# Weighing of the normed rows for the second half of the heads as three fp32r products, with the softmax sums of that slot behind its scores

## The reference

```
h1 = adaln(x, t, norm1_w, norm1_b)
x = mha(h1, h1, attn1_wq, attn1_wk, attn1_wv, attn1_wo, attn1_bo) + x
h2 = adaln(x, t, norm2_w, norm2_b)
x = mha(h2, context, attn2_wq, ...) + x
h3 = adaln(x, t, norm3_w, norm3_b)
x = glu_ff(h3, ff_w1, ff_b1, ff_w2, ff_b2) + x
...
def mha(xq, ctx, wq, wk, wv, wo, bo):
    scores = einsum('bhqd,bhkd->bhqk', q, k) / sqrt(DH)
    attn = softmax(scores, axis=-1)
    out = einsum('bhqk,bhkd->bhqd', attn, v)
    return out.transpose(0, 2, 1, 3).reshape(b, sq, INNER) @ wo + bo
...
attn = softmax(q[..., :, None] * k[..., None, :], axis=-1)   # router of the expert layer
logits = einsum('bsej,bsj->bse', attn, v)
```

## Time and profile before

| | us |
|---|---|
| median of 3 runs | 2139.29 |
| lowest and highest | 2135.04, 2143.15 |
| the profiled execution, its own time | 2140.15 |
| its span in the trace | 2138.4 |
| PE busy | 2045.5 (96%) |
| DVE, ACT, POOL busy | 1321.4, 1394.0, 1071.4 |
| one round of the loop (chunk to chunk in the trace, the PE of 1016.64 to 1121.52) | 104.88 |
| mean granted clock of TensorE, share of full | 0.989 |

### The profile page before, as it was taken

How to read it: one execution, slowest core, us unless ns; L and a number is a source line. 1 busy time by engine, 2 the same in 40 slices (tenths; PEclk the granted TensorE clock), 3 DMA queues, 4 the chain that set the end, 5 groups by cost and what they waited for, 6 DMA issues and landing times. The chain is left out here.

```text
span 2138.4 us, 38742 instructions
## 1 busy us (share of the span) xinstructions
PE 2045.5 (96%) x11068; PEld 1339.2 (63%) x11068; DVE 1321.4 (62%) x3389; ACT 1394.0 (65%) x2665; POOL 1071.4 (50%) x1198
## 2 busy tenths in 40 slices
PE   7899999999999999999999999999999888799996
PEld 5455555555555556555555555555565557699996
DVE  5554657676767666666666666666666555455565
ACT  4566666676767676767676767676766656666663
POOL 2434443636373737373737373737364355456654
PEclk9999999999999999999999999999999999999998
DMA  5110111111111111111212121111112212122266
GB/s 152 45 25 25 50 35 50 46 50 47 52 44 49 44 49 44 50 48 48 53 42 59 34 59 40 53 48 46 50 50 74 73 54 59 48 55 71 62 186 211
DMA packets 136322, 127.36 MB, mean 60 GB/s; under 512 B 14665, under 2 KB 110569, under 8 KB 136234
## 3 DMA queue, kind: packets, MB, share of 16 engines
q1 hardware_dynamic: 127466, 109.11, 18.5%
q0 software_dynamic: 8768, 17.20, 2.5%
HBM read 86.63 MB, written 40.67 MB: 60 GB/s over the span
## 5 line engine op out<-in xcount | busy, mean ns | idle before, releaser
L1882 POOL TENSOR_TENSOR pr<-pr,sm 128x512 f32<-128x512 f32 x256 | 277.6, 1097 | 484.9 <-DVE sm L1428 484.9
L1105 ACT ACTIVATE kp<-ps 128x512 f32<-128x512 f32 x512 | 298.9, 601 | 179.5 <-PE ps L283 175.0
L823 PE MATMUL ps<-tt,V 128*128 128x512 f32 x768 | 382.0, 595 | 3.5 <-ACT tt L1105 3.5
L1418 DVE TENSOR_REDUCE mx<-ps 128x8 f32<-128x512 f32 x256 | 176.8, 691 | 308.1 <-PE ps L772 308.1
L1105 ACT ACTIVATE tt<-ps 128x512 f32<-128x512 f32 x512 | 275.2, 591 | 40.2 <-PE ps L802 40.1
L772 PE MATMUL ps<-kp,hf 128*64 128x256 f32 x2048 | 279.3, 394 | 5.3 <-DVE pr L1421 2.4
L283 PE MATMUL ps<-cT,M 128*128 128x512 f32 x768 | 262.1, 464 | 0.0
L772 PEld LDWEIGHTS ps<-kp,hf 128*64 128x64 f32 x2048 | 125.4, 137 | 196.7 <-DVE pr L1421 140.2
L1105 ACT ACTIVATE pt<-ps 128x512 f32<-128x512 f32 x256 | 153.6, 600 | 143.0 <-PE ps L784 140.7
L283 PE MATMUL ps<-hk,M 128*128 128x512 f32 x768 | 242.2, 438 | 0.0
L929 PE MATMUL ps<-xT,wt 128*128 128x128 f32 (+1 forms) x1728 | 221.4, 278 | 9.5 <-DVE wt L1709 5.0
(11 more groups left out here) (229 smaller groups left out, 3477.2 us busy)
## 6 DMA issues: line engine op xcount, KB each, us to landing
mod<-emb_s SPq DMA_DIRECT2D x96, 256.0 KB, 4.2
xr<-rows_s SPq DMA_DIRECT2D x144, 66.0 KB
cb<-y_s SPq DMA_DIRECT2D x32, 256.0 KB
x_in<-in_x_dram SPq DMA_DIRECT2D x16, 256.0 KB, 4.3
xn_s<-x_in SPq DMA_DIRECT2D x16, 256.0 KB, 2.1
res<-xn_s SPq DMA_DIRECT2D x16, 256.0 KB, 2.8
c_in<-in_ctx_dram SPq DMA_DIRECT2D x16, 256.0 KB, 4.8
y_s<-res SPq DMA_DIRECT2D x16, 256.0 KB, 2.0
```

The lines of the kernel that those rows point to most:

```text
L823: mm = nc.tensor.matmul(psO[:], Vw[a][:, g * HG + head_at(h), :], tt[:, h, :], start=(g == 0 and h == 0), stop=ends)
L1105: return nc.scalar.activation(o, i, ACT.Copy)
L1418: nc.vector.tensor_reduce(mx[:, p % 2, :], heads(psS[p % 2][:]), AX_X, ALU.max).then_inc(max_done, 1)
L1882: tensor(v, v, sm[:, p, :].unsqueeze(2).broadcast_to([P, HG, 64]), ALU.mult).then_inc(prob_done, 1)
```

## The change

The weighing of unit 1 (in slot 2, for all chunks but the last) is done as three fp32r products instead of one fp32 product. For this, pt and h_tm are needed as an upper and a lower part each:

- ACT copies psT to pt_hi (fp32r) where it copied to pt. DVE makes the lower part, pt_lo = psT - pt_hi (`turn_rest`), once for each of the four steps, ahead of `peak` of the same step. psT is free only after that, so `turn` of steps 1 to 3 waits for pt_rest instead of pt_done.
- In slot 0, ACT makes a second copy of h1 (h_hl, upper part) and DVE the lower part (`tm_lower`, at h = 3).
- PE: lower h x pt_hi, upper h x pt_hi, upper h x pt_lo, each for both halves of the rows.
- In slot 2, none of the four `total` stands in the first part any more; they stand at h = 0, 1, 2 and 3.
- In the table of slot 2, `ln_lo(c, 2)` goes from h = 3 to h = 2 and `router_sum` from h = 2 to h = 3. At one h the jobs of the table stand ahead of `total`.

```diff
+            h_hl = sb("h_hl", [P, 2, NT, D], F32R, halves)
+            pt_hi, pt_lo = (sb(f"pt_{k}", [P, 2, CT], F32R, halves) for k in ("hi", "lo"))
...
+        def in_halves(i, u):
+
+            return u == 1 and not c_last(i)
+
+        def turned(i, u, p):
+
+            return (pt_rest, 4 * i + p + 1) if in_halves(i, u) else (pt_done, 4 * seq(i, u) + p + 1)
...
             def turn(i, u, p):
 
                 n = 4 * seq(i, u) + p
-                if not (isinstance(n, int) and n < 1):
+                if p:
+                    wait(turned(i, u, p - 1))
+                elif not (isinstance(n, int) and n < 1):
                     pe.wait_ge(pt_done, n)
...
                 pst = pstw[p % 2]
+                if in_halves(i, u):
+                    if p == 0:
+                        pe.wait_ge(tm_rest, i + 1)
+                    for k, of in enumerate((1, 0)):
+                        for s in range(2):
+                            rows = slice(64 * s, 64 * s + 64)
+                            nc.tensor.matmul(pst[s][:], h_hl[rows, of, p, :], pt_hi[rows, p % 2, :], start=k == 0, stop=False)
+                    pe.wait_ge(pt_rest, 4 * i + p + 1)
+                    for s in range(2):
+                        rows = slice(64 * s, 64 * s + 64)
+                        nc.tensor.matmul(pst[s][:], h_hl[rows, 0, p, :], pt_lo[rows, p % 2, :], start=False, stop=True).then_inc(t_done, 1)
+                    return
...
-                copy(pt[:, p % 2, :], psT[:]).then_inc(pt_done, 1)
+                copy((pt_hi if in_halves(i, u) else pt)[:, p % 2, :], psT[:]).then_inc(pt_done, 1)
...
                 copy(h_tm[:], h1[:]).then_inc(tm_done, 1)
+                if not c_last(c):
+                    copy(h_hl[:, 0], h1[:]).then_inc(tm_done, 1)
...
+            def turn_rest(i, u, p):
+
+                dve.wait_ge(pt_done, 4 * seq(i, u) + p + 1)
+                tensor(pt_lo[:, p % 2, :], psT[:], f32(pt_hi[:, p % 2, :]), ALU.subtract).then_inc(pt_rest, 1)
+
+            def tm_lower(c):
+
+                if not c_last(c):
+                    dve.wait_ge(tm_done, 2 * c + 2)
+                    tensor(h_hl[:, 1], h1[:], f32(h_hl[:, 0]), ALU.subtract).then_inc(tm_rest, 1)
...
+                early = 0 if last and in_halves(li, lu) else EARLY
                 for p in range(NT):
                     if u == 2 and p == 2 and ok(i - 3):
                         router_peak(i - 3)
+                    if last and in_halves(li, lu):
+                        turn_rest(li, lu, p)
                     if here:
                         peak(i, u, p)
...
-                    if p >= 4 - EARLY and here:
-                        total(i, u, p + EARLY - 4)
+                    if p >= 4 - early and here:
+                        total(i, u, p + early - 4)
...
-                hooks = {0: ((5, 1, context), (7, 3, after_glu)),
+                hooks = {0: ((3, 0, tm_lower), (5, 1, context), (7, 3, after_glu)),
...
-                    if h < NT - EARLY and here:
-                        total(i, u, h + EARLY)
+                    if h < NT - early and here:
+                        total(i, u, h + early)
```

More of the change, by code:

```diff
@@ L119, in pixart_block_moe @@
         RAWS = 4
+        with ExitStack() as halves:
+            h_hl = sb("h_hl", [P, 2, NT, D], F32R, halves)
+            pt_hi, pt_lo = (sb(f"pt_{k}", [P, 2, CT], F32R, halves) for k in ("hi", "lo"))
         raw_1 = sb("raw_1", [P, RAWS, 6, P])
@@ L232, in pixart_block_moe @@
         sum_done, rec_done, prob_done = sem("sum_done"), sem("rec_done"), sem("prob_done")
-        T_done, pt_done = sem("T_done"), sem("pt_done")
+        T_done, pt_done, pt_rest, tm_rest = sem("T_done"), sem("pt_done"), sem("pt_rest"), sem("tm_rest")
         t_done, tt_done = sem("t_done"), sem("tt_done")
@@ L791, in weigh @@
                 if p == 0 and u == 0:
-                    pe.wait_ge(tm_done, i + 1)
+                    pe.wait_ge(tm_done, 2 * i + 1)
                 if p == 0 and u == 2:
@@ L996, in next_key @@
                         if last:
-                            for w in [(pt_done, 4 * seq(li, lu) + 4)] if bank is psT else [] if bank in psS else t_free(li, lu, 3 if bank is psH else 2):
+                            for w in [turned(li, lu, 3)] if bank is psT else [] if bank in psS else t_free(li, lu, 3 if bank is psH else 2):
                                 wait(w)
@@ L1031, in slot @@
                     if last:
-                        pe.wait_ge(pt_done, 4 * seq(li, lu) + 4)
+                        wait(turned(li, lu, 3))
                     turn4(psT, back1, lambda k: oT[:, k * P:(k + 1) * P])
@@ L1476, in ln1_mod @@
                     dve.wait_ge(hx[0], c)
-                    dve.wait_ge(tm_done, c)
+                    dve.wait_ge(tm_done, 2 * c)
                 for t in range(NT):
@@ L1759, in stats3 @@
                     ln_stats(2, c, tmp)
-                hooks = {0: ((5, 1, context), (7, 3, after_glu)),
+                hooks = {0: ((3, 0, tm_lower), (5, 1, context), (7, 3, after_glu)),
                          1: ((3, 2, after_attn2), (4, 2, stats3), (6, 2, norm3), (8, -1, ln1_stats)),
-                         2: ((2, 3, router_sum), (4, 3, router_dot), (3, 2, lambda c: ln_lo(c, 2)), (4, -1, ln1), (6, 2, lambda c: glu_mul(c, 0)), (7, 2, lambda c: glu_split_lo(c, 0)), (8, -1, lambda c: ln_lo(c, 0)), (8, 3, top_first)),
+                         2: ((2, 2, lambda c: ln_lo(c, 2)), (3, 3, router_sum), (4, 3, router_dot), (4, -1, ln1), (6, 2, lambda c: glu_mul(c, 0)), (7, 2, lambda c: glu_split_lo(c, 0)), (8, -1, lambda c: ln_lo(c, 0)), (8, 3, top_first)),
                          3: ((0, 3, top_second), (1, 3, counts), (3, 0, after_attn1), (4, 0, stats2), (place_bank(i - 3)[2], 3, place_out), (6, 3, gates), (7, 0, norm2))}[u]
```

## The result

The changed kernel takes 2156.61 us, median of 6 runs (2153.39 to 2158.17), beside 2138.53 of the kernel before (6 runs, 2135.04 to 2143.15): a ratio of 1.0083 with a 95% interval of 1.0069 to 1.0098. It is slower, by 18 us, where 16.8 were forecast (2156.1 over 2139.3). The profiled executions have spans of 2156.4 and 2138.4, so their difference is the same 18.0, and the traces can be set side by side.

A forecast was written before the change was run, and what follows sets the result against it. PE, busy 96% of the span, was taken as the bound. 2140.15 + 15.6 (late `ln1`) - 0.1 (rounds 1 and 2) + 1.3 (round 0) = 2156.95, less 0.86 to the median: 2156.1 us, range 2151 to 2163.

The forecast's parts named there:

- PE has no hole to lose here: In slot 2 of a loop round, PE was taken as busy all of the 25.44 us, at full clock.
- The weighing: On PE in slot 2: each takes 0.88 us instead of 1.05, saving 0.68 a slot and 10.2 over 15 slots.
- The rival of the loads between the pairs: On PE, two weight loads show in each weighing, 13 to 18 us more, 2169 to 2174; chance 0.09.
- The second wait for psT: In slot 2, PE waits behind DVE's subtraction: 0.62 us at `turn` of step 1, 0.20 at step 3.
- The first part of the slot: Slot 2: the waits for psT less the shorter weighings, 0.62 + 0.20 - 0.68 = +0.14 us.
- `ln1`: Slot 2, rounds 3 to 14: late first norm delays PE's transposes 1.3 us (1.08 to 1.45) a round, 15.6 in all.
- the 0.37 that I allowed: On DVE, POOL's `prob` holds the first L1457 of `ln1`, which ends at 1087.6 instead of 1087.24.
- the first rival: Between `ln_lo` and L1482 on DVE: `ln1` still in time, delay within 1.65 us of slack, 2137 to 2150; chance 0.29.
- slot 0: Extra ACT copy (0.6 us) and DVE subtraction there: costed at nothing, up to 0.3 a round, 4 us.
- Round 0: Three `turn`s up to 0.77 us later each, less three shorter weighings: taken as 1.3 us.
- halves in turn: On PE, the fp32r row halves don't run side by side: 41 us more, 2197; chance 0.04.

The follow-up runs named there:

- the split alone: Changed kernel with the table and totals of before, so only the split into three fp32r products: 2144.26 us, ratio 1.0005.

## Why the prediction was right

*What bounds.* "PE has no hole to lose here" held: each wait that appeared went to the total, and the 3.4 us of PE's work that were saved are not to be seen in it.

*The weighing.* 0.88 was forecast from an fp32 record and an fp32r product of before; 0.89 was measured, and 0.15 a weighing by the trace in which it was taken back. The halves run side by side. The rival of the loads between the pairs fell. For it the Trainium skill, TensorE: Matmul & The Clock Gate, Part 3 (packing small matmuls), had been cited, by which a load overlaps a running product only when its row group is another. The trace doesn't agree: the loads of the third pair lie at 1079.18 to 1079.37, the second pair of products starts at 1079.17 and the third at 1079.40, 0.23 behind it, which is the length of an fp32r product. So both halves of the rows are in use while both are loaded anew, and no time is added.

*The second wait for psT.* Forecast 0.62 at step 1, 0.20 at step 3; measured 0.55 (1.57 less 1.02) and 0.04 (1.06, from 1082.22 to 1083.28, less 1.02). The first part of the slot came out at -0.08 instead of +0.14. What was mis-sized at step 3 is DVE's queue: I added the full times of `peak`, `router_peak` and `turn_rest`, but each of the last two starts about 0.08 ahead of the end of the one before it (`router_peak` at 1082.22, where the subtraction of `peak` ends at 1082.30; `turn_rest` 0.33 behind it, where `router_peak` takes 0.41). At step 1 it is the handovers, 0.03 and 0.06 where I took 0.08 twice. From DVE's timeline:

```profile
1082.22 0.41 DVE L1589 TENSOR_REDUCE oT<-oT 128x32 f32<-128x256 f32 x1
1082.55 0.68 DVE L1453 TENSOR_TENSOR pt_lo<-ps,pt_hi 128x512 fp32r<-128x512 f32 x1
```

*`ln1`.* `ln_lo` to the end of `ln1` was forecast at 7.08 to 7.44 and measured at 7.36; `router_dot` waits for `router_mul` as said, and L1457 is held (1.22 instead of 1.02, the lower half of the 0.37 that I allowed). ident,h is 1.05 later than before; the forecast was 1.3, of which 0.22 is the first part of the slot. Per round 1.15 instead of 1.3, so 13.8 us instead of 15.6. That the totals with the new table are the cause is shown by themselves alone (+1.16), and that it goes by way of POOL by the run in which `router_mul` stands ahead and `prob` behind `ln1` (+0.12). The slack was 1.91 and not the 1.65 of the first rival, as said above; the sum of the forecast, which counts from 1086.30, is not touched by that.

*What I had wrong.* Of slot 0 I wrote "I cost it at nothing, and up to 0.3 a round if the cover is thin". In the loop the nothing holds (the split alone drifts by -0.035 a round). In round 1 the second copy of h1 cost 0.5 us of waiting, shown by moving it, and in this execution 1.6 us of half clock behind it, which others with the same wait don't have; the prediction had no term for the clock. Round 0 itself came out as forecast: from its first `turn` to the first product with V it takes 73.85 to 83.74, 9.89 us, where it took 74.33 to 82.93, 8.60; 1.29 for a forecast of 1.3. The first two of its three waiting `turn`s, to be held against the earlier trace rows (the third waits 0.52 as the second does):

```profile
75.86 0.66 PE L797 MATMUL ps<-ident,pr 128*128 128x128 f32 x4 [1.41 <-DVE pt_lo L1453]
...
77.93 0.66 PE L797 MATMUL ps<-ident,pr 128*128 128x128 f32 x4 [0.52 <-DVE pt_lo L1453]
```

So the first rounds cost 3.3 and not 1.2 in this execution. This error and that of `ln1` have opposite signs (+2.1 and -1.8), and that the total of 2156.6 is so near to 2156.1, nearer than the steps are to theirs, is luck. What isn't luck is the main term: the chain, its wait for POOL and its length.

*The rivals.* `ln1` in time: fell, ident,h waits 0.98. Loads between the pairs and halves in turn: fell, the weighing takes 0.89.

## To carry to other kernels

An instruction moved back on one engine is to be followed through every engine that hands its result on: here two sums of 0.79 us on DVE cost PE next to nothing directly (0.12 a round with POOL out of the way), but the product that stood behind them on POOL came 3 us later. Removing one wait of a chain tells little where POOL and DVE work on the same stretch; ask what runs beside the freed instruction in its new place. And where a wait goes, count again what stands between each pair of handovers, since the order that closes one gap opens the next. And before a fall of the clock is laid to an edit, look for it in every profile that has the edit.

## What the runs showed of the hardware

- A TENSOR_SCALAR in SBUF that starts beside a POOL instruction ends 0.08 us behind it, and the next one can be held by the next POOL instruction. Four of them took 1.02 us with POOL idle, 1.22 where a `prob` ran on for 0.37 behind the start of the first, 1.73 where one ran on for 0.87, and 2.39 where POOL's instructions followed each other for 1.79. A TENSOR_REDUCE of the totals beside `prob` took 0.68 us (L1464 at 1092.38), against 0.63 at the lowest. The Trainium skill, SBUF — State Buffer, SBUF: two separate sides, says that the port pair which DVE and GpSimd share is locked for a whole instruction by whoever starts first; the rows agree for TENSOR_SCALAR and for a subtraction of two operands in SBUF (1.40 against 0.69, with 0.85 of a `prob` still to run), and the reduction takes no part in it.
- PE idle for 1.36 or 1.37 us in round 1 went on at a granted clock of 1.00 in all five profiles. Idle for 1.86 to 1.89 in the same place, it went on at 1.00 in three profiles and fell to 0.50 in four, where nine fp32r products took 3.34 to 3.89 us instead of 2.31.
- Six fp32r products of half the rows, in pairs, take 0.89 us; one fp32 product for each half 1.05.
